# A two-layer graph network on one core: turning the normalised rows of groups 1 to 7 through DRAM by transposing DMAs instead of on TensorE

## What is computed

```
Wh    = x @ W.T                                   # layer 0
norms = norm(Wh, axis=1)
sim   = Wh @ Wh.T / (norms * norms.T + 1e-8)
alpha = softmax(where((adj > 0) | eye(N), sim, -inf), axis=1)
x1    = layernorm(x + alpha @ Wh)
mask  = (adj > 0)                                 # layer 1
agg   = mask @ x1 / max(sum(mask, 1), 1)
out1  = concat(x1 @ W_self + b_self, agg @ W_nb + b_nb) @ W_comb + b_comb
out   = layernorm(x1 + relu(out1))
```

## Time and profile before

| | |
|---|---|
| median of 3 runs | 901.79 us (901.3 to 901.96) |
| the profiled execution's own time | 900.57 us |
| its span, first to last instruction | 898.8 us |
| PE (TensorE matmuls) busy | 877.6 us, 98% |
| DVE (VectorE) busy | 588.0 us, 65% |
| ACT (ScalarE) busy | 391.1 us, 44% |
| POOL (GpSimd) busy | 64.2 us, 7% |
| granted TensorE clock, mean | 0.998 |

### The profile page before, as it was taken

How to read it: one execution, slowest core, us unless ns; L and a number is a source line. 1 busy time by engine, 2 the same in 40 slices (tenths; PEclk the granted TensorE clock), 3 DMA queues, 4 the chain that set the end, 5 groups by cost and what they waited for, 6 DMA issues and landing times.

```text
span 898.8 us, 20852 instructions
## 1 busy us (share of the span) xinstructions
PE 877.6 (98%) x7151; PEld 711.1 (79%) x7151; DVE 588.0 (65%) x1265; ACT 391.1 (44%) x661; POOL 64.2 (7%) x175
## 2 busy tenths in 40 slices
PE   7989999999999999999999999999999999999997
PEld 6857777687777777787777777777888888888886
DVE  3787788887766777668868777889816333333333
ACT  4955655565665656565556665555310000000000
POOL 2300000000000000000000000011101000000000
PEclk9999999999999999999999999999999999999999
DMA  9226455465555654567558559584773213312200
GB/s 243 99 83 172 131 170 147 122 192 159 145 153 160 192 149 145 168 175 187 162 145 229 148 157 305 160 223 109 207 115 115 96 43 112 113 50 80 112 19 18
DMA packets 143213, 128.29 MB, mean 143 GB/s; under 512 B 64225, under 2 KB 120834, under 8 KB 142114
## 3 DMA queue, kind: packets, MB, share of 16 engines
q1 hardware_dynamic: 143058, 127.20, 49.5%
q0 software_dynamic: 80, 0.13, 0.1%
HBM read 95.83 MB, written 25.18 MB: 135 GB/s over the span
## 4 chain that ended last, share of the span: by engine, by line
issue 87%; POOL 5%; PE 4%; DMA 1%; DVE 1%; POOLq 1%; ACT 0%; SPq 0%; DVEq 0%
POOL rstd L527 3%; PE ps L1061 3%; POOL var_eps L525 1%; DMA feat<-xT 1%; PE ps L1073 1%; PE ps L1116 0%; POOLq L526 0%; PE ps L1143 0%; DVE work L692 0%; POOLq L524 0%; DVE work L807 0%; ACT prob_hi L593 0%; DVE big L685 0%; DVE mix_extremes L764 0%; POOLq L529 0%
## 5 line engine op out<-in xcount | busy, mean ns | idle before, releaser
L1165 PE MATMUL ps<-feat,prob_hi 128*128 128x257 f16 (+1 forms) x1024 | 279.8, 273 | 0.0
L1167 PE MATMUL ps<-feat,prob_lo 128*128 128x257 f16 (+1 forms) x1024 | 279.5, 273 | 0.0
L1166 PE MATMUL ps<-feat,prob_hi 128*128 128x256 f16 (+1 forms) x1024 | 278.9, 272 | 0.0
L839 DVE SCALAR_TENSOR_TENSOR prob_lo<-work,prob_hi 128x512 f16<-128x512 f32 x256 | 175.9, 687 | 82.1 <-ACT prob_hi L593 79.7
L1298 PE MATMUL ps<-big,mgroup 128*128 128x257 f16 x1024 | 226.2, 273 | 0.0
L1299 PE MATMUL ps<-big,mgroup 128*128 128x256 f16 x1024 | 226.2, 273 | 0.0
L593 ACT ACTIVATE prob_hi<-work 128x512 f16<-128x512 f32 x256 | 154.5, 624 | 91.2 <-DVE work L832 46.0
L586 ACT ACTIVATE work<-ps 128x512 f32<-128x512 f32 (+2 forms) x144 | 79.5, 556 | 138.1 <-PE ps L1095 120.6
L598 ACT ACTIVATE mask<-work 128x1024 fp8e4<-128x1024 f32 x128 | 133.5, 1043 | 0.0
L1166 PEld LDWEIGHTS ps<-feat,prob_hi 128*128 128x128 f16 x1024 | 100.3, 98 | 25.1
L1165 PEld LDWEIGHTS ps<-feat,prob_hi 128*128 128x128 f16 x1024 | 100.0, 98 | 24.2 <-issue 0.3
(11 more groups left out here) (121 smaller groups left out, 788.9 us busy)
## 6 DMA issues: line engine op xcount, KB each, us to landing
adj_sb<-adjT SPq DMA_DIRECT2D x128, 512.0 KB, 3.8
mask_spill<-mask SPq DMA_DIRECT2D x128, 128.0 KB, 2.7
mgroup<-mask_spill SPq DMA_DIRECT2D x8, 2048.0 KB, 8.3
xres<-x SPq DMA_DIRECT2D x8, 512.0 KB, 5.0
x1h_dram<-big SPq DMA_DIRECT2D x16, 256.0 KB, 5.2
out<-rows SPq DMA_DIRECT2D x32, 128.0 KB, 1.7
feat<-xT SPq DMA_DIRECT2D x7, 512.0 KB, 5.8
norm_bc<-norm_row_dram SPq DMA_DIRECT2D x8, 256.0 KB, 4.9
```

The source lines that it names most:

```text
L839: dve.scalar_tensor_tensor(out=prob_lo[:, s, :], in0=prob[:, s, :], scalar=PROB_SCALE, in1=prob_hi[:, s, :], op0=ALU.mult, op1=ALU.subtrac ...
L1165: pe.matmul(acc(D + 1), prob_hi[:, s, cols], feat_hi_of(g)[:, r, 0:D + 1], start=start, stop=False)
L1166: pe.matmul(acc(D), prob_hi[:, s, cols], feat_lo_of(g)[:, r, :], start=False, stop=False)
L1167: return pe.matmul(acc(D + 1), prob_lo[:, s, cols], feat_hi_of(g)[:, r, 0:D + 1], start=False, stop=stop)
```

## The change

Only group 0 is still turned on TensorE, and VectorE copies both halves of it out of PSUM (`unitT_out`, lines 728 and 729 of the changed kernel). The halves of groups 1 to 7 are stored to DRAM and loaded turned. They lie in the upper four groups of `feat` (`UNIT_SLOTS`), so the column of ones of groups 4 to 7, which lies there too, is written only after all seven stores have landed. The tails of groups 6 and 7 (`PROMPT` = 6) move into the pairs (0, 1) and (0, 2), and so do their stores. The squares of group 7 read PSUM and its copy waits for them. SP's loads of phase 0 have another order, `norm_row` comes later, and the banks of the small matmuls change.

```diff
-        unit = work[:, 4 * GW:8 * GW].bitcast(F16).rearrange("p (r h b d) -> p r h b d", r=2, h=2, b=GB)
+        def unit_of(g):
+            return feat[:, G // 2 + g % UNIT_SLOTS, 0:2 * GB * D].rearrange("p (h b d) -> p h b d", h=2, b=GB)
...
+            def store_units(g):
+                sync.wait_ge(unit_ready, g + 1)
+                sync.dma_start(unit_dram[g].rearrange("h (b p) d -> p h b d", p=P), unit_of(g)).then_inc(unit_stored[g], 16)
+
+            def load_unitT(g):
+                sync.wait_ge(unit_stored[g], 16)
+                for half, to in enumerate((unitT_hi, unitT_lo)):
+                    sync.dma_start_transpose(to[:, :, g * GW:(g + 1) * GW], unit_dram[g, half]).then_inc(unitT_loaded[g], 16)
 
             for g in range(4, G):
                 sync.wait_ge(wh_done, g - 3)
                 load_xT(g)
+                if g == 4:
+                    load_setup()
+                if g == 5:
+                    load_direct(0, 0, 0, 0)
+                    load_direct(0, 0, 1, 1)
+            for g in range(1, PROMPT):
+                store_units(g)
+                if g > 1:
+                    load_unitT(g - 1)
             load_unit(0, 1, 0, 2)
             load_unit(0, 1, 1, 3)
+            load_unitT(PROMPT - 1)
...
                 diagonal(a)
+                if a == 0:
+                    pair(0, 1, False)
+                    store_units(PROMPT)
+                    pair(0, 2, False)
+                    store_units(PROMPT + 1)
+                    load_unitT(PROMPT)
+                    pair(0, 3, False)
+                    load_unitT(PROMPT + 1)
...
             def unit_heads(g):
 
                 act.wait_ge(norm_ready, g + 1)
-                wait(act, unitT_done, g - 1)
+                act.wait_ge(wh_copied, g + 1)
+                if g == UNIT_SLOTS:
+                    act.wait_ge(unitT_done, 1)
+                if g > UNIT_SLOTS:
+                    act.wait_ge(unit_stored[g - UNIT_SLOTS], 16)
...
-                if g == G - 2:
-                    setup_out(0, mixw[:, 0:KD, :].rearrange("p k n -> p (k n)"), 3, KD * D)
-                if g == G - 1:
-                    setup_out(1, mixw[:, KD:2 * KD, :].rearrange("p k n -> p (k n)"), 1, KD * D)
-                unitT_out(g - 1)
...
             copy_wh(0)
             copy_wh(1)
             for g in range(G):
-                if g + 2 < G:
+                if g + 2 < G - 1:
                     copy_wh(g + 2)
-                if g < G - 1:
+                if g < PROMPT:
                     unit_tails(g)
+                if g + 2 == G - 1:
+                    copy_wh(G - 1)
+                if g == 1:
+                    unitT_out()
                 if g == 2:
                     widen_biases()
-                if 0 < g < G - 1:
-                    unitT_out(g - 1)
...
-            dve.tensor_copy(norm_row[:, :], ps[0:NB, 2, 2 * P:3 * P]).then_inc(norms_copied, 1)
             dve.wait_ge(scales_done, 1)
-            dve.tensor_copy(scales[:, :], ps[:, 2, 3 * P:3 * P + 2]).then_inc(scales_ready, 1)
-            unit_tails(G - 1)
+            dve.tensor_copy(scales[:, :], ps[:, 6, 0:2]).then_inc(scales_ready, 1)
             dve.wait_ge(scales_ready, 1)
...
+                    if late is not None and j == 5:
+                        unit_tails(late)
...
                 if a == 0:
                     between = [weight_scales, lambda: split_weights(0), lambda: split_weights(1)]
+                    for g in range(1, G):
+                        dve.wait_ge(unit_stored[g], 16)
+                    for g in range(G // 2, G):
+                        dve.memset(feat_hi_of(g)[:, :, D:D + 1], 1.0)
...
-            for g in range(4):
+            for g in range(G):
                 project(g)
-            for g in range(G - 4):
-                turn_units(g)
-                project(g + 4)
-            turn_units(G - 4)
+                if g == 3:
+                    turn_units()
```

More of the change, by code:

```diff
@@ L50 @@
 EARLY = 4
+UNIT_SLOTS = 4
+PROMPT = 6
 EPS_MATTERS_BELOW = 0.5
@@ L259, in gnn_program @@
         unitT_done = sem("unitT_done")
-        unitT_hi_ready = sem("unitT_hi_ready")
-        unitT_lo_ready = sem("unitT_lo_ready")
+        unitT_ready = sem("unitT_ready")
+        unit_stored = [sem(f"unit_stored{g}") for g in range(G)]
+        unitT_loaded = [sem(f"unitT_loaded{g}") for g in range(G)]
         bias_wide_ready = sem("bias_wide_ready")
@@ L366, in _, with load_setup @@
[L366 to L370, removed]
+            def load_setup():
+                sync.dma_start(w_selfT_sb, w_selfT.rearrange("(k p) n -> p k n", p=P)).then_inc(setup_loaded, 16)
+                sync.dma_start(w_nbT_sb, w_nbT.rearrange("(k p) n -> p k n", p=P)).then_inc(setup_loaded, 16)
+                sync.dma_start(w_comb_sb, w_comb.rearrange("(k p) n -> p k n", p=P)).then_inc(setup_loaded, 16)
+                with nc.allow_non_contiguous_dma(reason="biases as columns, the diagonal: single elements"):
+                    sync.dma_start(bias_col[:, 0:KD], b_self.rearrange("(k p) -> p k", p=P)).then_inc(setup_loaded, 16)
+                    sync.dma_start(bias_col[:, KD:2 * KD], b_nb.rearrange("(k p) -> p k", p=P)).then_inc(setup_loaded, 16)
+                    sync.dma_start(bias_comb[:, :], b_comb.rearrange("(a n) -> a n", a=1)).then_inc(setup_loaded, 16)
+                    sync.dma_start(adj_diag[:, :], adj_diag_v).then_inc(diag_loaded, 16)
@@ L922, in diagonal @@
                     mask_diagonal(a, t0 + j, f0 + j, j, u, u % 4, 16 * (u // 4 + 1))
-                    if a == 0 and j == 0:
-                        unitT_out(G - 1)
                     if j:
                         tails(t0 + j - 1, j - 1)
+                    if a == 0 and j == 1:
+                        dve.wait_ge(norms_turned, 1)
+                        dve.tensor_copy(norm_row[:, :], ps[0:NB, 2, 0:P]).then_inc(norms_copied, 1)
                     if between and 0 < a < G - 1 and j < GB - 1:
@@ L929, in diagonal, with pair @@
                 tails(t0 + GB - 1, GB - 1)
-            def pair(a, b, first, between):
+            def pair(a, b, first, between, late=None):
                 t0, f0, u0 = (before + more for before, more in zip(tiles_before(a), (GB, GB, 2)))
@@ L1063, in project, with turn_units @@
                 ins.then_inc(wh_done, 1)
[L1065 to L1069 removed]
+            def turn_units():
+                pe.wait_ge(unit_ready, 1)
                 for half in range(2):
@@ L1072, in turn_units @@
                         for k in range(KD):
-                            ins = pe.transpose(unitT_ps(g % 2, half)[:, k, b * P:(b + 1) * P],
-                                               unit[:, g % 2, half, b, k * P:(k + 1) * P], ident16[:, :])
+                            ins = pe.transpose(unitT_ps(half)[:, k, b * P:(b + 1) * P],
+                                               unit_of(0)[:, half, b, k * P:(k + 1) * P], ident16[:, :])
                 ins.then_inc(unitT_done, 1)
@@ L1248, in _ @@
                 if a == 0:
-                    pair(0, 1, False)
-                if a < G - 2:
-                    with pe.Fori(max(a + 1, 2), G - 1) as b:
+                    for b, needed in ((1, (2,)), (2, (3, 4, 5)), (5, (6, 7))):
+                        for g in needed:
+                            pe.wait_ge(unitT_loaded[g], 32)
+                        if b == 2:
+                            with pe.Fori(2, 5) as b:
+                                pair(0, b, False)
+                        else:
+                            pair(0, b, False)
+                    pair(0, 6, False)
+                elif a < G - 2:
+                    with pe.Fori(a + 1, G - 1) as b:
                         pair(a, b, False)
```

89 lines of the change are left out of this document (39 added, 50 removed).

## The result

| | kernel before | changed kernel |
|---|---|---|
| median, first comparison | 901.99 us (12 runs, 900.68 to 903.44) | 903.22 us (12 runs, 901.33 to 904.33) |
| median, second comparison, beside the experiments | 901.04 us (15 runs, 899.98 to 901.99) | 901.27 us (11 runs, 899.89 to 903.37) |
| ratio, first | | 1.0020 (95%: 1.0011 to 1.0028) |
| ratio, second | | 1.0004 (95%: 0.9995 to 1.0013) |
| profiled executions: own time, span | 900.57, 898.8 us | 904.33, 902.5 us; in the second comparison 900.10, 898.3 us |

The forecast was +0.9 us; measured are +1.2 and +0.2. By the bound of 0.2% the first comparison lies on the edge of "the same" (its interval does not hold 1) and the second inside. The first profile of the changed kernel is the slowest of its 12 runs, and the profile of before was a quick one: the 3.7 us between their spans are not what the change costs.

A forecast was written before the change was run, and what follows sets the result against it. TensorE was taken to bound the kernel from 69 us on, chains through several engines before it. −9.6 + 1.3 + 7.2 + 2.0 = +0.9 us gave 901.5, or 902.7 us for the median; range 898.5 to 906.0.

The forecast's parts named there:

- The start: From phase 0 into the attention, until TensorE is full: 9.6 us earlier, with ends 8.4 and 10.2.
- Step (1): Phase 0, TensorE: its 0.95 us wait for group 4's features goes, and four groups of 3.51 end at 35.0.
- Step (4): Start of attention: scale copied at 42.1 instead of 49.13, first exponential at 42.9 instead of 49.37.
- Step (5): VectorE after the scale: only group 0's features remain before the first mask, at 44.3, 9.1 us earlier.
- Step (6): Between first mask and first tails: a turned copy of 0.6 goes, `norm_row` takes 0.3 back; 9.6 us earlier taken overall.
- Tails 6: Pair (0, 1): 1.6 us of VectorE work before tile 6's mask, of which 1.3 reach TensorE (0.8 to 1.6).
- The end of pair (0, 2): Tails 7 and VectorE's wait for store 7, landing taken as 4.5 us, delay TensorE by 7.2 us (5.8 to 9.5).
- The clock: After TensorE's new hole, from about 101.0 to 107.8: coming out at half clock costs 2.0 us (0 to 2.2).
- The hole is short: Rival: store lands in 3.1 us, TensorE returns at full clock or nearly so, 899.3 us; chance 0.20.
- The store is slow: Rival: store 7 lands in 6.8 us behind other queue traffic, 905.0 us, deciding from a 5.4 landing; chance 0.14.
- The wait is not felt: Rival: VectorE passes the wait without a hole in TensorE, only two tails count, 894.8 us; chance 0.06.
- phase 0 gains less: Rival: late load of group 4 or 5, or late turned groups; 3 us of 9.6 missing, 905.7 us; chance 0.10.

The follow-up runs named there:

- the late wait: Changed kernel with VectorE's wait for the seven stores and its four memsets moved one pair later, behind pair (0, 3): 893.53 us, ratio to the kernel before 0.9917.
- the tails' experiment: On top of the late wait, the tails of groups 6 and 7 moved from tile 5 to tile 3 of their pairs: 891.91 us, ratio to before 0.9896.
- again: Second profile of the changed kernel, unchanged, run on the second chip beside the experiments: own time 900.10 us, median of its runs 901.27 us.
- the experiment that filled the hole: Changed kernel, wait left in place, with 28 matmuls into a free score bank while TensorE waits before pair (0, 3): 899.36 us, ratio to before 0.9984.

## Why the prediction was right, point by point

- **What bounds.** That every hole in TensorE past 69 us costs its length held for the large one: the late wait took away the hole and its clock and gave back 8.1 to 9.1 us (7.9, and the 0.2 or 1.2 of the changed kernel), where 7.7 were expected; in the ledger the hole and the clock are 8.9 to 9.0, tails 7 among them. For a gain of 2 us or less it can't be said: of the 2.5 that the tails' experiment had at 180 us its profile kept 0.7.
- **The start, 9.6.** Step (1), the wait for group 4 gone and four groups done at 35.0: 35.6. Step (2), squares 7 ended at 37.6: 38.2. Step (3), extremes at 39.85: 40.19. Step (4), scale 42.1 and first exponential 42.9: 42.33 and 43.22 in the first profile, 41.54 and about 42.1 in "again". ("Again" was ahead of the forecast so far, with 34.8 in step (1) and 39.40 in step (3).) Step (5), the mask at 44.3: 45.31, and 44.85 in "again". This is the step that was mis-sized: from the scale to the mask 2.2 us were counted, and it took 3.0 and 3.3. Behind the features stood no work but VectorE's read of the flag, 0.71 us with nothing to release it (1.05 in "again"), which I had not counted; the rows of before show no idle time at that read. Step (6), 9.6 in all: 7.3 in the first profile, 9.3 in "again". Between the two lies the granted clock in the diagonal, which the prediction had not seen coming: in the first profile the lead shrank from 8.6 at the tails (46.70) to 7.3 at the third tile's transposes, in "again" it went from 9.1 (46.24) to 9.3. The other half a microsecond is from the start of phase 0: TensorE's first four groups ended at 20.84 in the first profile and at 20.05 in "again", of which the longer gap at the flag took 0.3 back. What the order of the loads, the missing copies and the moved tails each give of the 9.6 was read from rows; no run separates them, except for the squares.
- **Tails 6, 1.3:** 1.3 in both profiles. That they could have been free where VectorE idles, the tails' experiment shows in its rows; by the medians it is worth 1.2, with overlapping intervals.
- **The end of pair (0, 2), 7.2:** 7.4 and 7.2. The landing, taken as 4.5 between 3.1 and 6.8, was 4.7 and 4.5. VectorE's idle time of 5.5 was foretold as 5 to 6, and the memset's place, near 95 us, was 98.67 and 96.49. The estimate of 3.5, worked out from figures of the Trainium skill's "DMA: Bandwidth & Descriptors", was too short; the skill's fixed cost of about 2.0 us stands there under "Anatomy of one DMA — SWDGE (gpsimd) path", for DMAs that GpSimd issues, and this store is SyncE's. The Trainium skill's rule to wait late ("DMA: Bandwidth & Descriptors", "Rules for kernel authors") is what the first experiment followed; the trace agrees, with 7.9 us below before.
- **The clock, 2.0:** 1.6 and 1.7 in the profiles, and 1.6 by the pitch in the experiment that filled the hole. The mechanism held and the size was a little high: it had been taken from a whole group of phase 0 at half clock, while here the clock was full again, or nearly (in "again"), by the next transposes.
- **The rivals.** "The hole is short" falls, as the landing was 4.7 and the clock fell. "The store is slow" wanted a landing of 5.4 or more. "The wait is not felt" falls with the wait of 6.6 us. Of "phase 0 gains less" neither cause came: no load of a group was late, and TensorE waited for no turned group. The first profile lost 2.3 of its 3 us all the same, for the most part by another way, the clock in the diagonal.
- **The number.** 902.7 forecast for the median, 903.22 and 901.27 measured. The lower bound of the sum was added up wrongly: −10.2 + 0.8 + 5.8 + 0 is −3.6 and not −3.1; the range does not hang on it. That the sum rests on compensations, −9.6 against +10.5, was the forecast's real content, and the late wait shows both halves: the gain is there once the loss is taken away.

## What to carry to other kernels

When a change frees an engine that is not the bound and adds a wait elsewhere, look for what is queued behind the waiting instruction: here one wait for a store of 512 KB, placed before work that TensorE needed, cost 8 to 9 us and ate a gain of the same size, while the same wait one pair later cost nothing. Count a hole in TensorE of the size seen here (3.9 and 6.4 to 6.6 us) as its length and then the half clock behind it, and look at every read of a value by an engine: it left up to 1.1 us of idle time here, and none in the kernel before. Two profiles of one kernel can differ by more than the change is worth, so set the median beside any profile before reading a difference of 2 or 3 us in it.

## What the runs showed of the hardware that was not expected

- The granted clock fell not only in long holes. In the first diagonal TensorE was idle for 0.39, 0.50 and 0.56 us between 45 and 47.5 us in the first profile, and the clock read 0.50 from 48 to 50 us; in "again", with idle times of 1.14 and 0.56 there, it stayed at 1.00. It fell in the diagonal of three of the eight profiles that have the turning DMAs (the first, the late wait, the tails at tile 3) and not in the other five, two of them with nine short transposes there. What decides it was not found. With those transposes it was very likely at full there in all nine executions: their mean clock is 0.999 or 1.0, and a fall as in the late wait's profile, some 1.7 us of clock lost in 892, would leave 0.998 at most.
- A DMA that turns 256 KB held SyncE's queue for 1.2 to 3.6 us (for example 2.50 at 94.33), a plain load or store of 512 KB mostly for 0.4 to 0.6, a few up to 1.3. No engine was seen to wait for it here.
- Reading a flag into VectorE's registers left 0.7 to 1.1 us in which the engine waited for nothing that the profile shows, and moving the read moved the gap; in the kernel before no such gap is seen at the same read.
